# Graph attention on one core: the weights-row gathers moved behind the last residual of A on GpSimd's queue, and the B matmuls made to wait for them in four groups

## The chip, the cores and the metric

The kernel runs on one core of a Trainium2 chip. The metric is device time in microseconds (us) of the whole launch. Three runs of the kernel before took 432.70, 432.72 and 432.77 us, so the median is 432.72 us. Five compute engines work side by side, each with its own queue of instructions, and meet only at semaphores: TensorE (PE, with its weight loads shown apart as PEld), VectorE (DVE), ScalarE (ACT), GpSimd (POOL) and SyncE (SP), which here only starts DMAs. GpSimd starts DMAs too, the indirect ones, which gather rows by a table of indices.

## The reference

There are 2048 nodes with 128 features. `X` is 2048 x 128, `A` is 2048 x 2048.

```python
XW = X @ W
s_col = XW @ a[0, :f];  s_row = XW @ a[0, f:]
den = exp(leaky_relu(s_row[:, None] + s_col[None, :], 0.01))
num = A @ den
att = where(num != 0, den / num, 0)
H = A @ (att @ XW)
out = layernorm(x + H)
```

## The kernel before, in words

The kernel sorts the nodes by their row score and, apart from that, by their column score. `den` is then a staircase: for most pairs of a block of rows and a block of columns, leaky_relu is linear, and the product with `A` splits into sums that need only a few coefficients. Only the blocks on the staircase's edge are multiplied out in full.

**Stage A** brings in `A` transposed, in the sorted order of its rows, as 32 half blocks of 128 x 1024 values in 32 bits (the code calls their number `n`, block `b = n // 2`, half `h = n % 2`; the text here says "half 23" and so on). Each half goes through four steps:

- GpSimd issues an indirect DMA that gathers it into one of the 11 places of a ring (L233, `fetch`). Half `n + 11` is fetched only once half `n` has left its place.
- ScalarE casts it to 16 bits, into `Ahi` (L432, semaphore `hi_done`).
- The residual, the half minus `Ahi`, goes into `Alo`: for two halves of three on VectorE (L718, `lo_dve`), and for every third (`n % LOS == LOS - 1` with `LOS = 3`, so halves 2, 5, ..., 20, 23, 26, 29) on GpSimd (L244, `lo_pool`). This is what "a residual of A" is in the title.
- TensorE multiplies it by `E`, in six matmuls a half (L347), after `wait_lo(pe, n)`, which wants the residuals of all halves up to `n`. That sum is `ps`, later `sums`.

`Alo` and `Ahi` of blocks 12 to 15 (halves 24 to 31) lie where the ring's places were. So the cast and the residual of these halves also wait until the places are vacated (`wait_vacated`): the casts of halves 24 and 25 want all residuals up to 22, those of 26 and 27 want them up to 24, those of 28 and 29 up to 26, and those of 30 and 31 up to 28. The residuals of 24 and 25 want them up to 21, of 26 and 27 up to 23, of 28 and 29 up to 25, of 30 and 31 up to 27. "Up to" takes in those on GpSimd.

**Stage C** begins when TensorE is through with half 31. It has 64 steps `t = 4 * J + c`, of 16 blocks `J` and 4 column parts `c`. In a step TensorE forms `num` (L379, L384, L386: two matmuls with `sums` and, between them, usually six with `Ahi`, `Alo` and `D`), ScalarE takes square, logarithm and exponential (L484, L486, L477), VectorE forms the leaky_relu, subtracts the logarithm and multiplies to give `att` (L738, L755, L746). Three steps later TensorE adds `xws[J]` times `att` to `B` (L357, in `add_bt(t)`; a matmul in 32 bits, which the trace shows as two). `xws` holds the rows of `XW` in the order of the column scores, 128 of them for each `J`. They are gathered from the scratch tensor `d_xw` in HBM by 16 indirect DMAs on GpSimd (L260), one for each `J`.

After stage C the 16 blocks of `B` are scattered back to HBM in the order of the row scores (L268, GpSimd), read again, and multiplied by `A` (L407). Then come the layernorm and the store.

What sets the order: each engine runs its queue in the order in which the code writes it. GpSimd has one queue for the fetches, its residuals, the gathers of L260 and the scatters of L268. In the loop over `n` the gathers stand at `n = 21` to `28` (`XWG = 21`), two at each `n`.

Of the kernel before, what the change touches and what calls it, by code (L numbers as in the profile page):

```python
# [7 lines left out]
FEAT = 128  # L8
# [4 lines left out]
NB = NODES // P  # L13
# [1 line left out]
BATCH = tuple((s, min(s + NB // 2, NS)) for s in range(0, NS, NB // 2))  # L15
CROW = 4
STAIR = 8
XWG = 21
LOS = 3
LATE = 12  # L20
R = 96
# [15 lines left out]
def graph_attention_layernorm(nc, xT, x, adjT, w, wT, a2, cst, before, ids, out):  # L37
# [17 lines left out]
    NC = N // W  # L55
# [4 lines left out]
    with ctx:  # L60
        def sb(name, shape, dt=F32):
            return ctx.enter_context(nc.sbuf_tensor(name, shape, dt))

        def sem(name):
            return ctx.enter_context(nc.semaphore(name))

        def dram(name, shape, dt=F32):
            return nc.dram_tensor(name, shape, dt, kind="Internal").ap()
# [7 lines left out]
        xws = sb("xws", [P, N])  # L76
# [11 lines left out]
        perm = sb("perm", [P, 2, 3, NB], U32)  # L88
# [48 lines left out]
        RG = len(ring)  # L137
# [12 lines left out]
        d_xw = dram("d_xw", [N, FEAT])  # L150
# [6 lines left out]
        names = """in_w in_x in_c p_wa wa_sb p_row p_col r_even r_odd row_c rcol_sb ccol_sb p_xw xw_sb xw_out  # L157
            const ramp flags flags_used ranked_sb hots p_place perm_r perm_c thr hot p_pre cmax crow_t crow_sb
            slots_ready mask_ready hi_done lo_dve lo_pool e_zero e_ready p_sums sums_hi sums_sb
            m_ready e_exp v d_z d_lz d_exp d_lo w_exp w_m w_hi w_lo xws_in r01_sb shift_sb num_ready  # L160
            lz_ready sq_done ln_done sub_done exp_done att_ready bt_added bt_sb b_t b_sb b_out
            b_in0 b_in1 bhi_done blo_done ht ht_sb h_t x_in var std y_ready stored""".split()
        names += [f"g{i}" for i in range(RG)]
        S = {n: sem(n) for n in names}
        block = ctx.enter_context(nc.Block())

        def wait_lo(engine, n):

            engine.wait_ge(S["lo_dve"], n + 1 - (n + 1) // LOS)
            if n + 1 >= LOS:  # L170
                engine.wait_ge(S["lo_pool"], (n + 1) // LOS)

        def wait_vacated(engine, n, part):

            if n // 2 >= LATE:
                wait_lo(engine, n // 2 * 2 - (2 if part is Ahi else 3))
# [7 lines left out]
        @block.sync  # L184
        def _(sp):
            sp.dma_start(wTs[:, :], wT).then_inc(S["in_w"], 16)
            sp.dma_start(a2s[:, :], a2).then_inc(S["in_w"], 16)
            sp.dma_start(xTs[:, :], xT).then_inc(S["in_x"], 16)
            sp.dma_start(ws[:, :], w).then_inc(S["in_x"], 16)
            sp.dma_start(tri[:, :], before).then_inc(S["in_c"], 16)  # L190
            sp.dma_start(idt[:, :, :], ids).then_inc(S["in_c"], 16)
            sp.dma_start(cstt[:, :], cst).then_inc(S["in_c"], 16)
            sp.wait_ge(S["xw_sb"], 1)
            sp.dma_start(d_xw.rearrange("(b p) f -> p b f", p=P), stage[:, 0:N].rearrange("p (b f) -> p b f", b=NB)
                         ).then_inc(S["xw_out"], 16)

            sp.wait_ge(S["bt_added"], NB * NC)
            sp.dma_start(xs.rearrange("p (b f) -> p b f", b=NB), x.rearrange("(b p) f -> p b f", p=P)).then_inc(S["x_in"], 16)

            sp.wait_ge(S["b_out"], 16 * NB)  # L200
            for g in range(2):
                sp.dma_start(Bs[:, g * N // 2:(g + 1) * N // 2].rearrange("p (b f) -> p b f", b=NB // 2),
                             d_b.rearrange("(b p) f -> p b f", p=P)[:, g * NB // 2:(g + 1) * NB // 2, :]).then_inc(S[f"b_in{g}"], 16)
            for c in range(NC):
                sp.wait_ge(S["y_ready"], c + 1)
                sp.dma_start(out.rearrange("(b p) f -> p b f", p=P)[:, 4 * c:4 * c + 4, :],
                             y[:, 4 * c:4 * c + 4, :]).then_inc(S["stored"], 16)
            sp.wait_ge(S["stored"], 16 * NC)

        @block.gpsimd  # L210
        def _(pool):
            nc.gpsimd.memset(ident[:, :], 1.0).then_inc(S["const"], 1)
            nc.gpsimd.memset(epst[:, 0:1], EPS).then_inc(S["const"], 1)
            nc.gpsimd.memset(epst[:, 1:2], TINY).then_inc(S["const"], 1)
            nc.gpsimd.memset(E[:, :, :, :], 0.0).then_inc(S["e_zero"], 1)
            pool.wait_ge(S["const"], 3)
            nc.gpsimd.affine_select(out=ident[:, :], in_=ident[:, :], compare_op=ALU.is_equal, fill=0.0, base=0,
                                    pattern=[[-1, P]], channel_multiplier=1).then_inc(S["const"], 1)

            nc.gpsimd.iota(ramp16[:, :], pattern=[[1, N]], base=0, channel_multiplier=0,  # L220
                           allow_small_or_imprecise_dtypes=True).then_inc(S["ramp"], 1)
            nc.gpsimd.memset(onesb[:, :], 1.0).then_inc(S["const"], 1)
            pool.wait_ge(S["perm_r"], 1)

            rows = adjT.rearrange("k (h i) -> (k h) i", h=2)

            def fetch(n):
                b, h = divmod(n, 2)
                if n == RG - NG - 1:
                    pool.wait_ge(S["xw_out"], 16)  # L230
                if n >= RG:
                    wait_lo(pool, n - RG)
                nc.gpsimd.indirect_dma_start(  # L233
                    out=ring[n % RG], out_offset=None, in_=rows,
                    in_offset=bass.IndirectOffsetOnAxis(ap=perm[:, 0, h, b:b + 1], axis=0)).then_inc(S[f"g{n % RG}"], 16)

            for n in range(RG):
                fetch(n)
            for n in range(2 * NB):
                b, h = divmod(n, 2)  # L240
                if n % LOS == LOS - 1:
                    pool.wait_ge(S["hi_done"], n + 1)
                    wait_vacated(pool, n, Alo)
                    nc.gpsimd.tensor_tensor(Alo[:, b, h * H:(h + 1) * H], ring[n % RG], Ahi[:, b, h * H:(h + 1) * H],  # L244
                                            ALU.subtract).then_inc(S["lo_pool"], 1)
                if n + RG < 2 * NB:
                    fetch(n + RG)
                if n == STAIR + 1:

                    pool.wait_ge(S["mask_ready"], 1)  # L250
                    pool.wait_ge(S["w_exp"], 1)
                    w3 = tmp[0:R, :].rearrange("p (b j) -> p b j", b=NB)
                    nc.gpsimd.tensor_tensor(w3, w3, mask[0:R, :].unsqueeze(2).to_broadcast([R, NB, P]), ALU.mult
                                            ).then_inc(S["w_m"], 1)
                if n == XWG:
                    pool.wait_ge(S["perm_c"], 1)
                if XWG <= n < XWG + NB // 2:

                    for b in range(2 * (n - XWG), 2 * (n - XWG + 1)):
                        nc.gpsimd.indirect_dma_start(  # L260
                            out=xws[:, b * FEAT:(b + 1) * FEAT], out_offset=None, in_=d_xw,
                            in_offset=bass.IndirectOffsetOnAxis(ap=perm[:, 1, 2, b:b + 1], axis=0)).then_inc(S["xws_in"], 16)


            for b in range(NB):
                if b % 4 == 0:
                    pool.wait_ge(S["b_sb"], b // 4 + 1)
                nc.gpsimd.indirect_dma_start(  # L268
                    out=d_b, out_offset=bass.IndirectOffsetOnAxis(ap=ranku[:, b:b + 1], axis=0),
                    in_=Bn[:, b * FEAT:(b + 1) * FEAT], in_offset=None).then_inc(S["b_out"], 16)  # L270
# [8 lines left out]
        def _(pe):  # L279
# [5 lines left out]
            for i in (1, 0):  # L285
# [7 lines left out]
                for b in range(NB):  # L293
                    if i and b % 4 == 0:
                        h, c = divmod(b // 4, 2)
# [35 lines left out]
            for n in range(2 * NB):  # L331
# [11 lines left out]
                b, h = divmod(n, 2)  # L343
# [7 lines left out]

            def add_bt(t):
                J, c = divmod(t, NC)
                if c == 0:
                    pe.wait_ge(S["xws_in"], 16 * NB)
                pe.wait_ge(S["att_ready"], t + 1)
                nc.tensor.matmul(bt[c], xws[:, J * FEAT:(J + 1) * FEAT], att[c], start=(J == 0), stop=(J == NB - 1)  # L357
                                 ).then_inc(S["bt_added"], 1)
# [11 lines left out]
            for J in range(NB):  # L370
                lo, hi1 = ends_of(J)
                for c in range(NC):
                    t = J * NC + c
# [24 lines left out]
            for c in range(NC - LAG, NC):  # L398
                add_bt((NB - 1) * NC + c)
                transpose_b(c - 1)  # L400
# [113 lines left out]
        def _(dve):  # L514
# [170 lines left out]
            def leaky_relu(i):  # L685

                z, _, s1 = batch(i)
                dve.wait_ge(S["d_z"], s1)
                V.scalar_tensor_tensor(z, z, SLOPE, z, ALU.mult, ALU.max).then_inc(S["d_lz"], 1)
# [119 lines left out]
```

## Time and profile before

| | |
|---|---|
| median of three runs | 432.72 us |
| profiled execution, its own time | 432.18 us |
| its span, first to last instruction | 430.4 us |
| mean granted TensorE clock | 0.845 |
| TensorE matmuls busy | 296.5 us (69%) |
| VectorE busy | 251.3 us (58%) |
| ScalarE busy | 195.5 us (45%) |
| GpSimd busy | 103.1 us (24%) |
| indirect DMAs of L260: count, time from issue to landing | 16, 2.6 us |

The span is 430.4 us and the execution's own time 432.18 us, so 1.78 us lie around the span. The busy shares are averages over stages with different limits. GpSimd's 24% is nearly all in stage A and between C and the last product with `A`. The granted clock is that of TensorE as a share of 2.4 GHz: 1.00 is the upper of its two levels and 0.50 the lower, and a stretch with 0.7 has both in it.

### The profile page before, as it was taken

Reading aid. Unit: us, or ns where it says so; the run is one execution under the profiler, and the core shown is the slowest. Engines: PE = TensorE matmul, PEld = TensorE weight load, DVE = VectorE, ACT = ScalarE, POOL = GpSimd, SP = SyncE. Lnnn points to the kernel's source line nnn. Section 1 sums busy time; section 2 is a strip of 40 time slices with the busy share of each in tenths; the row PEclk is TensorE's granted clock in tenths of the full one; section 3 lists DMA queues with packets and bytes.
Section 4 is the critical chain, followed back from the end, with each engine's and each line's share of the span. In section 5 each row is a group of like instructions: output and inputs, shape, how many; then the busy total and the mean of one; then the engine's idle time right before and its main releaser. Section 6 shows DMA issues by size and latency. Waiting matters only on the chain.

```text
span 430.4 us, 5170 instructions
## 1 busy us (share of the span) xinstructions
PE 296.5 (69%) x1466; PEld 145.1 (34%) x1466; DVE 251.3 (58%) x468; ACT 195.5 (45%) x294; POOL 103.1 (24%) x86
## 2 busy tenths in 40 slices
PE   4863122863456555669999999999999700699950
PEld 2463111631122222324444444444444300244420
DVE  0759977477688413196888888876888500201036
ACT  1210013142697413187878787857878800100020
POOL 4000057563766788200000000000000174000000
PEclk9985555967588988689999999999999965699985
DMA  3030049732246511000000000000000052200002
GB/s 121 0 97 4 2 150 376 250 128 88 81 148 190 164 37 36 14 0 0 2 1 2 0 2 0 0 2 0 2 0 0 8 152 75 59 2 1 0 24 73
DMA packets 13445, 24.65 MB, mean 57 GB/s; under 512 B 1648, under 2 KB 8176, under 8 KB 13296
## 3 DMA queue, kind: packets, MB, share of 16 engines
q0 software_dynamic: 5632, 18.88, 13.5%
q1 hardware_dynamic: 7792, 5.50, 4.4%
q8 instruction: 12, 0.20, 0.2%
q14 instruction: 9, 0.07, 0.1%
HBM read 21.23 MB, written 3.15 MB: 57 GB/s over the span
## 4 chain that ended last, share of the span: by engine, by line
PE 51%; DVE 19%; POOL 12%; ACT 7%; issue 5%; DMA 4%; POOLq 0%; SPq 0%; ACTq 0%; DVEq 0%
PE ps L384 18%; PE ps L357 11%; PE ps L407 10%; POOL xws L260 4%; POOL d_b L268 3%; PE ps L347 3%; DVE Alo L718 2%; DVE D L547 2%; PE ps L290 2%; POOL Alo L244 2%; DVE D L549 2%; PE ps L379 2%; PE ps L386 2%; DMA Ahi<-adjT,perm 2%; ACT tmp L458 1%
## 5 line engine op out<-in xcount | busy, mean ns | idle before, releaser
L347 PE MATMUL ps<-Ahi,E 128*96 128x512 f16 x128 | 54.9, 490 | 53.9 <-POOL Alo L244 30.5
L384 PE MATMUL ps<-Ahi,D 128*128 x248 | 85.3, 383 | 0.7 <-issue 0.4
L357 PE MATMUL ps<-stage,xws 128*128 128x512 f32 x128 | 65.8, 595 | 3.7 <-DVE stage L746 3.7
L755 DVE TENSOR_TENSOR tmp<-crow,tmp 128x512 f32<-128x512 f32 x64 | 44.2, 691 | 30.4 <-ACT tmp L486 30.4
L407 PE MATMUL ps<-Ahi,D 128*128 128x512 f16 x128 | 39.7, 389 | 25.0 <-DVE D L763 25.0
L268 POOL DMA_INDIRECT d_b<-crow,ranku x16 | 15.4, 961 | 170.8 <-ACT crow L493 166.2
L484 ACT ACTIVATE tmp<-ps 128x512 f32<-128x512 f32 x64 | 38.0, 594 | 29.0 <-PE ps L386 29.0
L384 PE MATMUL ps<-Alo,D 128*128 x124 | 47.4, 382 | 0.0
L347 PEld LDWEIGHTS ps<-Ahi,E 128*96 128x96 f16 x128 | 19.9, 156 | 81.1 <-issue 57.0
L486 ACT ACTIVATE tmp<-tmp,epst 128x512 f32<-128x512 f32 x64 | 46.2, 722 | 2.1
L477 ACT ACTIVATE tmp<-tmp,ebias 128x512 f32<-128x512 f32 x64 | 45.3, 708 | 0.2 <-DVE tmp L755 0.2
L746 DVE SCALAR_TENSOR_TENSOR stage<-ps,tmp 128x512 f32<-128x512 f32 x64 | 43.7, 683 | 0.2 <-ACT tmp L477 0.2
L384 PEld LDWEIGHTS ps<-Ahi,D 128*128 x248 | 24.1, 97 | 44.0 <-issue 23.2
L347 PE MATMUL ps<-Alo,E 128*96 128x512 f16 x64 | 31.3, 489 | 0.0
L233 POOL DMA_INDIRECT Ahi<-adjT,perm x12 | 15.2, 1270 | 58.5 <-DVE rs L576 51.4
L407 PEld LDWEIGHTS ps<-Ahi,D 128*128 128x128 f16 x128 | 12.8, 100 | 40.8 <-DVE D L763 25.3
L407 PE MATMUL ps<-Alo,D 128*128 128x512 f16 x64 | 24.8, 388 | 0.0
L738 DVE SCALAR_TENSOR_TENSOR crow<-crow,shift,rrow 128x512 f32<-128x512 f32 x32 | 23.8, 742 | 0.1
L357 PEld LDWEIGHTS ps<-stage,xws 128*128 128x128 f32 x128 | 19.6, 193 | 12.1 <-issue 3.7
L738 DVE SCALAR_TENSOR_TENSOR crow<-stage,shift,rrow 128x512 f32<-128x512 f32 x32 | 23.7, 742 | 0.0
L432 ACT CAST Ahi<-Ahi 128x1024 f16<-128x1024 f32 x12 | 12.5, 1040 | 21.7 <-POOL Alo L244 17.8
L718 DVE TENSOR_TENSOR Alo<-Ahi 128x1024 f16<-128x1024 f32 x8 | 10.9, 1357 | 19.0 <-ACT Ahi L432 18.9
(166 smaller groups left out, 407.2 us busy)
## 6 DMA issues: line engine op xcount, KB each, us to landing
tmp<-xT SPq DMA_DIRECT2D x1, 1024.0 KB, 4.9
d_xw<-stage SPq DMA_DIRECT2D x1, 1024.0 KB, 5.1
xws<-d_b SPq DMA_DIRECT2D x2, 512.0 KB, 4.6
out<-crow SPq DMA_DIRECT2D x4, 256.0 KB, 2.3
xws<-d_xw,perm POOLq DMA_INDIRECT x16, 2.6
d_b<-crow,ranku POOLq DMA_INDIRECT x16, 2.2
Ahi<-adjT,perm POOLq DMA_INDIRECT x12, 5.4
Alo<-adjT,perm POOLq DMA_INDIRECT x11, 5.6
```

The costliest lines, as they stand in the source:

```text
L268: nc.gpsimd.indirect_dma_start(out=d_b, out_offset=bass.IndirectOffsetOnAxis(ap=ranku[:, b:b + 1], axis=0), in_=Bn[:, b * FEAT:(b + 1) * F ...
L347: mm = nc.tensor.matmul(ps[0:R, c, :], E[:, e, b, :], a[:, b, c * W:(c + 1) * W], start=(b == 0 and i == 0), stop=(b == NB - 1 and i == 2))
L357: nc.tensor.matmul(bt[c], xws[:, J * FEAT:(J + 1) * FEAT], att[c], start=(J == 0), stop=(J == NB - 1)).then_inc(S["bt_added"], 1)
L384: nc.tensor.matmul(num[c], D[:, d, bass.ds(slot, 1), :], a[:, bass.ds(k, 1), o:o + W], start=False, stop=False, skip_group_check=True)
L407: mm = nc.tensor.matmul(bt[c], B16[:, d, k, :], a[:, k, c * W:(c + 1) * W], start=(k == 0 and i == 0), stop=(k == NB - 1 and i == 2))
L477: nc.scalar.activation(L_t[c], L_t[c], ACT.Exp, bias=ebias[:, J:J + 1]).then_inc(S["exp_done"], 1)
L484: nc.scalar.activation(L_t[c], num[c], ACT.Square, scale=1.0 / 256).then_inc(S["sq_done"], 1)
L486: nc.scalar.activation(L_t[c], L_t[c], ACT.Ln, bias=epst[:, 1:2]).then_inc(S["ln_done"], 1)
L718: V.tensor_tensor(Alo[:, b, h * H:(h + 1) * H], ring[n % RG], Ahi[:, b, h * H:(h + 1) * H], ALU.subtract).then_inc(S["lo_dve"], 1)
L738: V.scalar_tensor_tensor(lz_t[t % 2], r01[c // 2][:, c % 2 * W:(c % 2 + 1) * W], shift[:, J:J + 1], rrow[:, c * W:(c + 1) * W], ALU.add, A ...
L746: V.scalar_tensor_tensor(att[c], num[c], 1.0 / 256, L_t[c], ALU.mult, ALU.mult).then_inc(S["att_ready"], 1)
L755: V.tensor_tensor(L_t[c], lz_t[t % 2], L_t[c], ALU.subtract).then_inc(S["sub_done"], 1)
```

## The change

The 16 gathers leave the loop over the halves and stand behind it, so that GpSimd issues them one after another when it is through with its last residual (half 29) and the loop. The semaphore `xws_in`, which counted all 16, becomes four, one for every four gathers (`XG = 4`). TensorE, which waited for all 16 at the first column part of every `J`, now waits at `J = 0, 4, 8, 12` for the group of that `J` alone.

```diff
-XWG = 21
+XG = 4
...
-        ... w_hi w_lo xws_in r01_sb ...
+        ... w_hi w_lo r01_sb ...
-        names += [f"g{i}" for i in range(RG)]
+        names += [f"g{i}" for i in range(RG)] + [f"xws_in{i}" for i in range(NB // XG)]
...
-                if n == XWG:
-                    pool.wait_ge(S["perm_c"], 1)
-                if XWG <= n < XWG + NB // 2:
-
-                    for b in range(2 * (n - XWG), 2 * (n - XWG + 1)):
-                        nc.gpsimd.indirect_dma_start(
-                            out=xws[:, b * FEAT:(b + 1) * FEAT], out_offset=None, in_=d_xw,
-                            in_offset=bass.IndirectOffsetOnAxis(ap=perm[:, 1, 2, b:b + 1], axis=0)).then_inc(S["xws_in"], 16)
-
+            pool.wait_ge(S["perm_c"], 1)
+            for b in range(NB):
+                nc.gpsimd.indirect_dma_start(
+                    out=xws[:, b * FEAT:(b + 1) * FEAT], out_offset=None, in_=d_xw,
+                    in_offset=bass.IndirectOffsetOnAxis(ap=perm[:, 1, 2, b:b + 1], axis=0)).then_inc(S[f"xws_in{b // XG}"], 16)
...
-                if c == 0:
-                    pe.wait_ge(S["xws_in"], 16 * NB)
+                if t % (NC * XG) == 0:
+                    pe.wait_ge(S[f"xws_in{J // XG}"], 16 * XG)
```

GpSimd's queue at the end of stage A, before. `L244` are its residuals (of halves 20, 23, 26 and 29 in this order), `L233` the fetches of halves of A, `L260` the gathers:

```order
L244 TENSOR_TENSOR Alo<-stage,Ahi 128x1024 [waits hi_done]
L233 DMA stage<-adjT,perm 128x1024 [waits lo_pool,lo_dve]
L260 DMA xws<-d_xw,perm 128x128 [waits perm_c]
L260 DMA xws<-d_xw,perm 128x128 x3
L244 TENSOR_TENSOR Alo<-Alo,Ahi 128x1024 [waits hi_done]
L260 DMA xws<-d_xw,perm 128x128 x6
L244 TENSOR_TENSOR Alo<-Ahi 128x1024 [waits lo_pool,lo_dve,hi_done]
L260 DMA xws<-d_xw,perm 128x128 x6
L244 TENSOR_TENSOR Alo<-stage,Ahi 128x1024 [waits lo_pool,lo_dve,hi_done]
```

The same place now, where the gathers are `L257` and the scatters of `B` that follow are `L264`:

```order
L244 TENSOR_TENSOR Alo<-stage,Ahi 128x1024 [waits hi_done]
L233 DMA stage<-adjT,perm 128x1024 [waits lo_pool,lo_dve]
L244 TENSOR_TENSOR Alo<-Alo,Ahi 128x1024 [waits hi_done]
L244 TENSOR_TENSOR Alo<-Ahi 128x1024 [waits lo_pool,lo_dve,hi_done]
L244 TENSOR_TENSOR Alo<-stage,Ahi 128x1024 [waits lo_pool,lo_dve,hi_done]
L257 DMA xws<-d_xw,perm 128x128 [waits perm_c]
L257 DMA xws<-d_xw,perm 128x128 x15
L264 DMA d_b<-crow,ranku 2048x128 [waits b_sb]
```

Between residuals 20 and 29 stood 4, 6 and 6 gathers; now the residuals follow one another, and all 16 gathers stand behind the last one. The fetch in front (of half 31, the last) did not move.

TensorE's queue where it adds `B` for the first column part of `J = 2`, before:

```order
L386 MATMUL ps<-sums,wgt 128x256
L357 MATMUL ps<-stage,xws 128x512 [waits att_ready,xws_in]
L367 TENSOR_LOAD lohi
L367 ISA x2
L368 TENSOR_LOAD lohi
L368 ISA x2
L379 MATMUL ps<-sums,wgt 128x256 [waits att_ready]
```

The same rows now (`L353` is the matmul into `B`):

```order
L382 MATMUL ps<-sums,wgt 128x256
L353 MATMUL ps<-stage,xws 128x512 [waits att_ready]
L363 TENSOR_LOAD lohi
L363 ISA x2
L364 TENSOR_LOAD lohi
L364 ISA x2
L375 MATMUL ps<-sums,wgt 128x256 [waits att_ready]
```

No matmul moved. The wait for the gathers is gone here, and at 12 of its 16 places; at the other four it names a group of four gathers.

## Rows read from the trace of the kernel before

**Rows 1.** The page, the chain that ended last, shares of the span by line:

```profile
PE ps L384 18%; PE ps L357 11%; PE ps L407 10%; POOL xws L260 4%; POOL d_b L268 3%; PE ps L347 3%; DVE Alo L718 2%; DVE D L547 2%; PE ps L290 2%; POOL Alo L244 2%; DVE D L549 2%; PE ps L379 2%; PE ps L386 2%; DMA Ahi<-adjT,perm 2%; ACT tmp L458 1%
```

**Rows 2.** Waits, 140 to 200 us (waiting line, awaited: us in total, times, longest):

```profile
PE ps L347 <- POOL Alo L244: 18.1, 4, 5.7
ACT Ahi L432 <- POOL Alo L244: 17.8, 3, 8.1
```

**Rows 3.** Timeline, GpSimd (start us, us, engine, line, instruction [idle before <-releaser]):

```profile
142.60 2.28 POOL L244 TENSOR_TENSOR Alo<-stage,Ahi 128x1024 f16<-128x1024 f32 x1
145.65 0.96 POOL L233 DMA_INDIRECT stage<-adjT,perm  x1 [0.77 <-POOL Alo L244]
...
151.88 2.14 POOL L244 TENSOR_TENSOR Alo<-Alo,Ahi 128x1024 f16<-128x1024 f32 x1
...
161.94 2.14 POOL L244 TENSOR_TENSOR Alo<-Ahi 128x1024 f16<-128x1024 f32 x1
164.24 0.96 POOL L260 DMA_INDIRECT xws<-d_xw,perm  x1 [0.16 <-issue]
...
168.86 1.96 POOL L260 DMA_INDIRECT xws<-d_xw,perm  x1 [0.30 <-issue]
...
173.32 2.14 POOL L244 TENSOR_TENSOR Alo<-stage,Ahi 128x1024 f16<-128x1024 f32 x1
```

**Rows 4.** Timeline, ScalarE and VectorE at the end of stage A:

```profile
147.21 1.22 DVE L718 TENSOR_TENSOR Alo<-Alo,Ahi 128x1024 f16<-128x1024 f32 x1
...
154.12 1.04 ACT L432 CAST Ahi<-Ahi 128x1024 f16<-128x1024 f32 x1 [7.14 <-POOL Alo L244]
...
156.15 1.23 DVE L718 TENSOR_TENSOR Alo<-Alo,Ahi 128x1024 f16<-128x1024 f32 x1 [7.72 <-ACT Ahi L432]
...
166.57 1.99 ACT L432 CAST Ahi<-stage 128x1024 f16<-128x1024 f32 x2 [0.39 <-issue]
...
167.64 2.36 DVE L718 TENSOR_TENSOR Alo<-stage,Ahi 128x1024 f16<-128x1024 f32 x2 [1.16 <-ACT Ahi L432]
```

**Rows 5.** Timeline, TensorE: matmuls after a short idle time, and where stage C starts:

```profile
122.08 0.42 PE L347 MATMUL ps<-Ahi,E 128*96 128x512 f16 x1 [1.28 <-DVE Alo L718]
...
145.03 0.39 PE L347 MATMUL ps<-Ahi,E 128*96 128x512 f16 x1 [2.87 <-POOL Alo L244]
...
148.70 0.38 PE L347 MATMUL ps<-Ahi,E 128*96 128x512 f16 x1
...
182.04 0.38 PE L347 MATMUL ps<-Ahi,E 128*96 128x512 f16 x1
...
189.78 1.10 PE L357 MATMUL ps<-stage,xws 128*128 128x512 f32 x2 [3.10 <-DVE stage L746]
```

**Rows 6.** Windows (stretch, its us, busy us and instructions of each engine, granted clock, DMA):

```profile
154.10:159.80 5.70, 5.61 (x18) 2.77 (x18) 1.23 (x1) 1.99 (x2) 4.41 (x5) 0.72 0.14 35
175.60:182.40 6.80, 6.80 (x19) 3.26 (x19) 0.82 (x2) 1.07 (x2) 0.00 (x0) 0.59 0.01 2
189.70:195.00 5.30, 4.78 (x11) 1.85 (x12) 4.32 (x7) 2.89 (x6) 0.00 (x0) 0.68 0.00 0
200.00:240.00 40.00, 40.00 (x170) 18.23 (x169) 32.73 (x51) 32.40 (x51) 0.00 (x0) 1.00 0.01 1
```

**Rows 7.** Timeline, 106 to 119 us: GpSimd and VectorE at the same time:

```profile
106.04 3.62 POOL L253 TENSOR_TENSOR tmp<-tmp,mask 96x2048 f32<-96x2048 f32 x1
107.41 3.33 DVE L718 TENSOR_TENSOR Alo<-Alo,Ahi 128x1024 f16<-128x1024 f32 x1 [2.60 <-ACT Ahi L432]
111.62 2.28 DVE L708 TENSOR_TENSOR wgt<-tmp,wgt 32x2048 f16<-32x2048 f32 x1 [0.87 <-ACT wgt L447]
112.61 3.27 POOL L244 TENSOR_TENSOR Alo<-Ahi 128x1024 f16<-128x1024 f32 x1 [0.61 <-ACT Ahi L432]
116.50 1.23 DVE L689 SCALAR_TENSOR_TENSOR tmp<-tmp 128x1024 f32<-128x1024 f32 x1 [2.60 <-ACT tmp L458]
116.66 1.90 POOL L233 DMA_INDIRECT Ahi<-adjT,perm  x1 [0.77 <-POOL Alo L244]
117.64 1.22 DVE L718 TENSOR_TENSOR Alo<-Alo,Ahi 128x1024 f16<-128x1024 f32 x1
```

**Rows 8.** The instructions of line L260, their transfers:

```profile
DMA to landing us min/median/max: 2.4/2.6/3.7
```

More of the change, by code:

```diff
@@ L159, in graph_attention_layernorm @@
             slots_ready mask_ready hi_done lo_dve lo_pool e_zero e_ready p_sums sums_hi sums_sb
-            m_ready e_exp v d_z d_lz d_exp d_lo w_exp w_m w_hi w_lo xws_in r01_sb shift_sb num_ready
+            m_ready e_exp v d_z d_lz d_exp d_lo w_exp w_m w_hi w_lo r01_sb shift_sb num_ready
             lz_ready sq_done ln_done sub_done exp_done att_ready bt_added bt_sb b_t b_sb b_out
             b_in0 b_in1 bhi_done blo_done ht ht_sb h_t x_in var std y_ready stored""".split()
-        names += [f"g{i}" for i in range(RG)]
+        names += [f"g{i}" for i in range(RG)] + [f"xws_in{i}" for i in range(NB // XG)]
         S = {n: sem(n) for n in names}
```

## The prediction

> **What bounds the kernel now.** I read the chain that ended last first. TensorE's lines of stage C and of the last product lead it, but one entry does not fit: the gathers of L260 hold 4% of the span, and GpSimd's residuals L244 another 2% [rows 1]. The gathers' data is first used in stage C, at 189.78 us, so their issue should be on no path. The waits from 140 to 200 us say how they come onto it: TensorE waits 18.1 us for residuals on GpSimd, and ScalarE's casts 17.8 us for the same [rows 2]. GpSimd's timeline closes the argument. After the fetch at 145.65 it has nothing before it but gathers, and the residuals of halves 23, 26 and 29 begin at 151.88, 161.94 and 173.32 only because they stand behind 4, 6 and 6 gathers [rows 3]. The next cast starts 0.10 us after the residual of half 23 is done (154.02), VectorE's next residual after the cast [rows 4]. So from 146.6 to 175.5 us GpSimd's queue bounds the kernel. From 182.42 us (the end of 182.04 + 0.38 [rows 5]) stage C follows, in which TensorE is busy 40.00 of 40.00 us [rows 6].
>
> **The change, part by part.**
>
> *Gathers out of the way.* The stretches that hold gathers are 146.61 to 151.88 (5.27 us), 154.02 to 161.94 (7.92) and 164.08 to 173.32 (9.24), 22.4 us together [rows 3]. They do not come back in full, since the casts and VectorE's residuals, which now run in their shadow, are late next. I follow them.
>
> Residual 23 is ready when the fetch ends, at 146.61; its cast is long done. Before, VectorE had the residuals of halves 24 and 25 until 148.43 [rows 4]. They now meet GpSimd's. The rows on such meetings: GpSimd's residual at 112.61 took 3.27 us instead of 2.14 and ended 1.98 us after VectorE's subtraction did (113.90); VectorE's residual at 107.41 took 3.33 instead of 1.22 and ended 1.08 after GpSimd's multiplication (109.66) [rows 7]. One waits for the other. Residual 24 on VectorE ends near 147.30 (25 begins 147.21), so residual 23 ends at 147.30 + 1.98 = 149.3 if it gets in between the two, and at 148.43 + 1.98 = 150.4 if it does not. With no such cost it would end at 146.61 + 2.14 = 148.75.
>
> The Trainium skill has this as a rule (SBUF — State Buffer, "Who interferes with whom"): VectorE's second read port is GpSimd's only one, and a VectorE instruction with two SBUF inputs and a GpSimd instruction that reads SBUF exclude each other for the whole instruction. The trace agrees, with the 3.27 and 3.33 us above. By the rule residual 23 ends at 149.3 or 150.4, and the case without a cost falls away.
>
> From there, in the later of the two cases: casts 26 and 27 from 150.5, 1.99 us for two [rows 4], so 151.5 and 152.5. Residual 26 on GpSimd from 151.6 to 153.7. VectorE's 27 waits for it and ends near 154.8. Casts 28 and 29 from 153.8 to 155.8. VectorE's 28 to 156.0. Residual 29 starts then on GpSimd and ends at 158.0. Casts 30 and 31 end at 157.2 and 158.1. VectorE's 30 waits for GpSimd and ends at 159.1, 31 at 160.3. All arrivals of halves are old: half 31 was issued at 145.65.
>
> TensorE needs (148.70 - 145.03)/17 = 0.216 us a matmul at the upper clock [rows 5], 1.30 for a half. It was done with half 22 at 149.08. From the end of residual 23 nine halves are left, 54 x 0.216 + 0.17 = 11.8 us. It would start half 26 at 154.3 (ready 153.7), 27 at 155.6 (154.8), 28 at 156.9 (156.0), 29 at 158.2 (158.0), 30 at 159.5 (159.1), 31 at 160.8 (160.3). Each is ready by 0.2 to 0.9 us, so TensorE itself is late next. It ends between 149.3 + 11.8 = 161.1 and 150.4 + 11.8 = 162.2. I take 161.8, nearer the later end, as the margins are thin. Against 182.42 that saves 20.6 us.
>
> *The clock.* The saving assumes 1.00 from 149 us on. Before, the clock stood at 0.72 for the halves after the first stall and 0.59 after the third [rows 6], each after 5 us or more without work. After 1.28 us (at 122.08), and even after 2.87 (at 145.03), TensorE went on with matmuls of 0.4 us, the upper level [rows 5]. Only one gap of 0.2 to 1.3 us is left here (149.08 to the end of residual 23). So I count the clock at nothing. If it falls all the same, the price is between 0 and 54 x 0.216 = 11.7 us; one stretch like that of 154.10 to 159.80, whose 18 matmuls took 5.70 us instead of 18 x 0.216 + 0.17 = 4.06, costs 1.6 us.
>
> *Gathers in their new place.* POOL is free of residual 29 at 157.0 to 158.0. A gather costs 0.96 us and 0.30 between two, so 1.26, but one that started under VectorE's residuals took 1.96 [rows 3]. Taking 2.26 for each, the fourth starts at 158.2 + 3 x 2.26 = 165.0 and lands after 2.6 to 3.7 us [rows 8], at 167.6 to 168.7. `add_bt(0)` came 189.78 - 182.42 = 7.36 us after the end of stage A [rows 5], which is now 169.2. The first group is in time by 0.5 to 1.6 us; at 1.26 a gather by over 4. VectorE's 51 instructions in 40 us, three a step, make 17 steps, 2.35 us each [rows 6]. So the second group is needed 16 steps later, near 207, and the sixteenth gather starts by 158.2 + 15 x 2.26 = 192.1. Cost 0. Above it: if gathers cost VectorE their own time at the start of C, where there is no slack, it is four times 0.96, 3.8 us. Nothing in the rows says so: residuals 30 and 31 took 2.36 for two with gathers under them [rows 4]. After that VectorE is busy 32.73 of 40 [rows 6] and can give 7 us in 40.
>
> *Fewer waits on TensorE.* Twelve waits go that were long fulfilled; the engine was busy 40.00 of 40.00 with them there [rows 6]. An engine without idle time has none to give back, and nothing is added that could cost. So 0.
>
> *The rest.* Stage C and what follows keep their lengths and move forward as a block. Its own half-clock stretch (0.68 from 189.70 to 195.00 [rows 6]) comes after the 3.10 us wait for the first `att`, which stays; it could change by 1.6 us either way.
>
> **Sum.** 432.18 - 20.6 = 411.6 for the profiled execution. The median of the runs is 0.54 higher, so 412.1.
>
> **Rivals.**
>
> *The clock falls in the closed-up end of stage A.* For it: at 0.2 us of margin a small delay makes gaps, and the clock was at 0.72 and 0.59 in these very halves. Against: the gaps of 1.3 us that did not lower it. One stretch gives 413.7, two 415.3, all nine halves at the lower level 412.1 + 11.7 = 423.8.
>
> *The first group is late or disturbs VectorE.* Four gathers of 2.26 and a late landing leave only 0.5 us. Another 1 to 4 us here gives 413 to 416.
>
> *Something else holds the casts.* If the casts of 26 to 31 need more than the residuals (an arrival, a place), half of the 20.6 would go: 422. The casts' only wait in the rows is GpSimd (17.8 us in 3).
>
> *Starved gathers, slower than before.* Gathers wait for VectorE (1.96 and 1.90 us). VectorE is busy 82% of stage C. If a gather only goes ahead when VectorE stands still for a while, none is issued until TensorE stops at the group's wait and VectorE runs dry. Then four go, 3 x 1.26 + 2.6 = 6.4 us, and four groups cost 25.6, against 20.6 saved: 437, and the clock's falls (1.6 us or more each) would bring it to 444. It decides from 5.15 us a group. Against it: at 116.66 an indirect DMA under two VectorE instructions back to back ended at 118.56, 0.83 after the first of them (117.73) and before the second (118.86) [rows 7]. It needs only the seam.
>
> The Trainium skill warns of this (SBUF — State Buffer, the "DVE blocks DMA" trap): GpSimd cannot write descriptors while VectorE is in a two-port performance mode. It excepts subtractions of two tensors. The trace differs in part, since the subtractions of L718 did delay a gather to 1.96 us. By the trap taken at its worst the time is that of the starved gathers; by the row it is the forecast.
>
> **How the numbers follow.** Forecast 0.74, with its own range of 410.3 to 414. Falling clock 0.13. First group 0.06. Something else 0.04. Starved gathers 0.03. The range 409.5 to 417 takes in the forecast, up to three lower-clock stretches and the late group, and on its lower side a stage C that starts without its half-clock stretch; it leaves out some 0.1. What a measurement of this kernel can tell from no change is about 0.2%, 0.9 us. Faster 0.96, the same 0.01, slower 0.03.
>
> **What would show it.** On GpSimd's timeline residuals 23, 26 and 29 end near 150, 154 and 158, with no gather between. The waits of TensorE for L244 after 145 us fall from 15 us to about 1. Stage C's first matmul stands near 161.8, the first matmul into `B` near 169 with its wait put down to VectorE and not to a DMA. The steps keep their 2.35 us. I am wrong if the clock is well below 1.00 between 150 and 162, if TensorE waits for VectorE's residuals there, or if a wait ends with a gather's landing.

## The result, and the profile after

The changed kernel takes 419.65 us (median of four runs, 419.47 to 420.14), the kernel before 432.71 us in the same session. The ratio is 0.9708, 95% interval 0.9686 to 0.9729. The gain is 13.1 us where 20.6 were forecast, and the time lies above the range given. The profiled execution took 419.58 us, with a span of 417.8.

GpSimd's timeline at the end of stage A, where lines carry new numbers (L257 is the gather, L264 the scatter, L343 TensorE's matmul of stage A, L353 the one into `B`, L375, L380 and L382 those of `num`, L480 ScalarE's square, L714 VectorE's residual). It answers to [rows 3]:

```profile
146.51 0.96 POOL L233 DMA_INDIRECT stage<-adjT,perm  x1 [0.77 <-POOL Alo L244]
147.49 2.13 POOL L244 TENSOR_TENSOR Alo<-Alo,Ahi 128x1024 f16<-128x1024 f32 x1
151.91 2.13 POOL L244 TENSOR_TENSOR Alo<-Ahi 128x1024 f16<-128x1024 f32 x1 [2.29 <-DVE Alo L714]
156.22 2.22 POOL L244 TENSOR_TENSOR Alo<-stage,Ahi 128x1024 f16<-128x1024 f32 x1 [2.18 <-ACT Ahi L428]
158.59 1.78 POOL L257 DMA_INDIRECT xws<-d_xw,perm  x1
...
178.83 0.94 POOL L257 DMA_INDIRECT xws<-d_xw,perm  x1 [0.30 <-issue]
```

The residuals follow one another within 11 us instead of 24, and the 16 gathers run behind them, from 158.6 to 179.8 us, one in 1.25 us. TensorE's waits from 140 to 163 us, which answer to [rows 2]:

```profile
PE ps L343 <- POOL Alo L244: 2.9, 1, 2.9
PE ps L343 <- DVE Alo L714: 1.4, 1, 1.4
```

The 18.1 us for GpSimd have become 2.9, and those lie ahead of half 20. Stage A's last matmul ends at 162.97 us (162.59 + 0.38). The first fetch of this execution began 0.89 us later than before (58.17 against 57.28). Counted from it, stage A ends after 104.8 us instead of 125.1, so 20.3 us are saved there.

Then stage C. The windows (stretch, its us, then busy us of TensorE, its weight loads, VectorE, ScalarE and GpSimd, granted clock, DMA) answer to [rows 6]:

```profile
163.00:170.30 7.30, 4.20 (x20) 1.91 (x20) 6.60 (x13) 7.20 (x12) 5.59 (x6) 1.00 0.18 47
170.30:182.50 12.20, 8.75 (x21) 2.43 (x22) 4.27 (x7) 3.72 (x7) 7.34 (x8) 0.72 0.19 48
190.00:230.00 40.00, 40.00 (x170) 18.14 (x168) 32.72 (x52) 32.47 (x51) 0.00 (x0) 1.00 0.00 1
```

In 12.2 us TensorE ran 21 matmuls, where some 50 are usual, and VectorE and ScalarE were busy for a third of it. What happened is in the timeline of TensorE and ScalarE:

```profile
172.05 0.71 ACT L473 ACTIVATE tmp<-tmp,ebias 128x512 f32<-128x512 f32 x1
...
173.79 0.63 PE L380 MATMUL ps<-Alo,D 128*128 x1
174.84 0.59 PE L380 MATMUL ps<-Ahi,D 128*128 x1 [0.41 <-issue]
175.57 0.37 PE L382 MATMUL ps<-sums,wgt 96*128 96x256 f16 x1 [0.15 <-issue]
...
178.81 0.63 PE L380 MATMUL ps<-Ahi,D 128*128 x1
181.17 0.60 ACT L480 ACTIVATE tmp<-ps 128x512 f32<-128x512 f32 x1 [8.41 <-remote]
181.26 0.38 PE L380 MATMUL ps<-Ahi,D 128*128 x1 [1.82 <-issue]
```

ScalarE's L480 of step 4 waits for the matmul L382 of that step. It ended at 175.94, and L480 began at 181.17, 5.2 us later; further on the same pair is 0.05 us apart (L382 ends at 186.70, L480 begins at 186.75). The ends of matmuls are modelled, but TensorE started several more behind this one, the last of them at 178.81, so it had long been done. "remote" is how the profile names a wait for which it finds no engine whose end released it. TensorE itself stutters: "issue" is idle time in which it waited for nothing shown. Both recover at 181.2, about when the last gather, issued at 178.83, should have landed by the 2.6 us of [rows 8] (an estimate, as this trace gives no landing for it). From stage C's first matmul to the first scatter of `B` it took 165.39 us (163.06 to 328.45) instead of 159.33 (182.32 to 341.65), so 6.1 us more. After that the steps are the old ones, 40.00 us busy of 40.00.

### The profile page after: what moved, and what is told of

It is laid out like the page before. It is cut to its first block, busy times and chain, and to the rows that moved or that the text cites. A ratio compares the mean times of both kernels' runs of the same rounds, so it can differ in the third digit from the quotient of the medians.

```text
span 417.8 us, 5158 instructions
## 1 busy us (share of the span) xinstructions
PE 295.9 (71%) x1466; PEld 143.9 (34%) x1466; DVE 255.3 (61%) x468; ACT 195.5 (47%) x294; POOL 102.1 (24%) x86
## 4 chain that ended last, share of the span: by engine, by line
PE 57%; DVE 22%; ACT 7%; POOL 5%; issue 5%; DMA 3%; POOLq 0%; SPq 0%; ACTq 0%; DVEq 0%
PE ps L380 20%; PE ps L353 12%; PE ps L403 10%; PE ps L343 5%; POOL d_b L264 3%; DVE Alo L714 3%; DVE D L543 2%; PE ps L286 2%; PE ps L375 2%; PE ps L382 2%; DVE D L545 2%; ACT tmp L454 1%; DVE tmp L685 1%; PE ps L297 1%; DVE D L559 1%
## 5 line engine op out<-in xcount | busy, mean ns | idle before, releaser
L380 PE MATMUL ps<-Ahi,D 128*128 x248 | 86.5, 386 | 2.9 <-issue 2.6
L343 PE MATMUL ps<-Ahi,E 128*96 128x512 f16 x128 | 50.6, 458 | 39.1 <-DVE Alo L714 25.4
L353 PE MATMUL ps<-stage,xws 128*128 128x512 f32 x128 | 67.0, 605 | 3.6 <-issue 2.9
L480 ACT ACTIVATE tmp<-ps 128x512 f32<-128x512 f32 x64 | 38.1, 595 | 35.2 <-PE ps L382 26.8
L264 POOL DMA_INDIRECT d_b<-crow,ranku x16 | 15.5, 970 | 153.3 <-ACT crow L489 148.7
L380 PE MATMUL ps<-Alo,D 128*128 x124 | 47.9, 386 | 0.4 <-issue 0.3
L380 PEld LDWEIGHTS ps<-Ahi,D 128*128 x248 | 24.2, 98 | 48.7 <-issue 28.1
L343 PEld LDWEIGHTS ps<-Ahi,E 128*96 128x96 f16 x128 | 18.5, 144 | 63.0 <-issue 35.3
L233 POOL DMA_INDIRECT Ahi<-adjT,perm x12 | 15.2, 1270 | 59.4 <-DVE rs L572 52.3
L343 PE MATMUL ps<-Alo,E 128*96 128x512 f16 x64 | 29.1, 455 | 0.0
L353 PEld LDWEIGHTS ps<-stage,xws 128*128 128x128 f32 x128 | 19.6, 193 | 11.5 <-issue 3.3
L503 ACT COPY rrow<-ps 128x512 f32<-128x512 f32 x4 | 2.3, 586 | 42.4 <-PE ps L403 42.4
L714 DVE TENSOR_TENSOR Alo<-Ahi 128x1024 f16<-128x1024 f32 x8 | 13.4, 1677 | 11.2 <-ACT Ahi L428 11.0
```

The source lines that it names most:

```text
L264: nc.gpsimd.indirect_dma_start(out=d_b, out_offset=bass.IndirectOffsetOnAxis(ap=ranku[:, b:b + 1], axis=0), in_=Bn[:, b * FEAT:(b + 1) * F ...
L343: mm = nc.tensor.matmul(ps[0:R, c, :], E[:, e, b, :], a[:, b, c * W:(c + 1) * W], start=(b == 0 and i == 0), stop=(b == NB - 1 and i == 2))
L380: nc.tensor.matmul(num[c], D[:, d, bass.ds(slot, 1), :], a[:, bass.ds(k, 1), o:o + W], start=False, stop=False, skip_group_check=True)
L480: nc.scalar.activation(L_t[c], num[c], ACT.Square, scale=1.0 / 256).then_inc(S["sq_done"], 1)
L714: V.tensor_tensor(Alo[:, b, h * H:(h + 1) * H], ring[n % RG], Ahi[:, b, h * H:(h + 1) * H], ALU.subtract).then_inc(S["lo_dve"], 1)
```

## The experiments

Two theories stood at the start. Theory 1: the gathers in flight hold up stage C. Theory 2: the place in the program does. The second run below paces the gathers; it is called the paced kernel, and most later runs build on it. The runs come from several sessions; the kernel before took 432.46 to 432.79 us in each, so their times are compared as they are.

**Plain load.** No gather on GpSimd.

```diff
+            sp.wait_ge(S["perm_c"], 1)
+            sp.dma_start(xws ..., d_xw ...).then_inc(S["xws_in0"], 16)
...
-            for b in range(NB):
-                nc.gpsimd.indirect_dma_start(out=xws..., in_=d_xw, ...)
```

> The changed kernel without any gather on GpSimd: xws is filled by one plain DMA on SyncE as soon as its place is free (it leaves out the sorting of the rows of XW). In the changed kernel ScalarE stands still from 172.8 to 181.2 us, TensorE's steps 4 and 5 are ragged, and both recover when the last gather must have landed (issued at 178.8). Theory 1, gathers in flight hold up the engines of stage C: the standstill is gone and the time is 419.65 - 6.5, so about 413, within 1 us of the 412.1 forecast. Theory 2, the standstill belongs to the place in the program (start of the second block J, where TensorE loads the loop bounds into registers and jumps): it stays, and the time is about 419.5.

412.44 us (411.03 to 413.13), ratio 0.9538 [0.9519, 0.9557]. No wait in stage C is "remote". This run leaves out the sorting of the rows. The standstill went with the gathers, and the forecast for the rest of the change holds.

**Paced groups.**

```diff
             for b in range(NB):
+                if b and b % XG == 0:
+                    pool.wait_ge(S["bt_added"], NC * b - 8)
```

> The changed kernel, with groups 1, 2 and 3 of the gathers held back on GpSimd until eight steps before TensorE needs them, so that only four gathers, over by about 166 us, run at the start of stage C and the others run in three bursts of 5 us later. Theory 1 in its simple form (any gather beside stage C costs): each burst shows its own standstill of some us, so about the 419.6 of the changed kernel, or more. Theory 1 with a threshold (only a long train of gathers builds something up, since the first ten ran beside stage C at no cost): no standstill, about 413. Theory 2 (place in the program): the standstill at step 4 stays, about 419.5.

411.40 us (410.66 to 411.88), ratio 0.9513 [0.9496, 0.9529]. This version does the whole work and is faster than both kernels, than the changed one by 8.2 us. Its windows of stage C, the second with the usual fall of the clock after the wait for the first `att`, the third with group 1 of the gathers in it:

```profile
161.50:169.00 7.50, 4.39 (x21) 2.15 (x22) 6.67 (x12) 7.40 (x12) 1.03 (x2) 1.00 0.07 20
169.00:182.00 13.00, 12.70 (x46) 5.16 (x45) 9.80 (x16) 9.26 (x16) 0.00 (x0) 0.87 0.00 0
182.00:200.00 18.00, 18.00 (x77) 8.24 (x76) 14.94 (x24) 14.46 (x23) 3.78 (x4) 1.00 0.05 15
```

TensorE is busy 18.00 of 18.00 us with four gathers beside it. So neither the place nor gathers as such cost anything; theory 2 falls, and theory 1 needs its threshold. Stage A ends 104.6 us after the first fetch (161.35 against 56.80), 20.6 us less than before.

**One wait for all 16**, the second part of the change undone:

```diff
-                if t % (NC * XG) == 0:
-                    pe.wait_ge(S[f"xws_in{J // XG}"], 16 * XG)
+                if c == 0:
+                    for g in range(NB // XG):
+                        pe.wait_ge(S[f"xws_in{g}"], 16 * XG)
```

> The changed kernel with the second part of the change undone: TensorE waits for all 16 gathers before the first matmul into B and at every block J, as before. The last gather lands at about 181.3, the first matmul into B stands at 170.3 now. If the wait alone counts, the time is 419.65 + 11 less the standstill of 6.5 that would lie inside this wait: about 424. If the standstill comes in addition, about 430. Under theory 2 the standstill comes after the wait, so 430.

424.63 us (two runs), ratio 0.9815 [0.9782, 0.9847]. The first matmul into `B`:

```profile
180.71 2.05 PE L354 MATMUL ps<-stage,xws 128*128 128x512 f32 x2 [14.67 <-DMA xws<-d_xw,perm]
```

It waits for the last gather and the standstill lies inside that wait, as the lower figure assumed. The groups are worth 5.0 us beside the new place of the gathers; against the 412.4 us of the plain load, where nothing stands still, they would be worth 12.2.

**Twelve gathers more**, into a place that nobody reads, behind the 16:

```diff
+            pool.wait_ge(S["p_sums"], 2)
+            for b in range(12):
+                nc.gpsimd.indirect_dma_start(out=spare[...], in_=d_xw, ...).then_inc(S["spare_in"], 16)
```

> The changed kernel with 12 more gathers of the same rows into a place that nobody reads, right behind the 16. GpSimd's train then ends at about 195 instead of 179.8. Theory 1: the standstill of ScalarE ends with the last landing, near 196.5, and the time grows by about 15, to 434. Theory 1 weaker (gathers slow the engines for a bounded time): 420 to 430. Theory 2: no change, 419.6.

435.92 us (434.16 to 438.42), 16.3 over the changed kernel, for a train 15 us longer. ScalarE's waits (us in total, times, longest):

```profile
ACT tmp L487 <- remote: 24.2, 3, 15.6
```

In the next runs the paced kernel carries something extra behind group 0, from about 163 us on.

**24 plain DMAs by SyncE** of as many bytes:

```diff
+            for k in range(24):
+                sp.dma_start(spare[...], d_xw[k % 12 * P:(k % 12 + 1) * P, :]).then_inc(S[f"sp_in{k % 12}"], 16)
```

> The paced kernel (411.4 us) and, from the start of stage C on, 24 plain DMAs of 64 KB each from the same scratch tensor, issued back to back by SyncE into a place that nobody reads. They bring as many bytes and as many completions as 24 gathers, with no work on GpSimd. Theory A (the traffic of the transfers and their completions on the semaphores hold up TensorE and ScalarE): a standstill as with a train of gathers, 425 us or more. Theory B (it needs GpSimd issuing the DMAs): no standstill, 411 to 413.

412.20 us. Theory A falls: neither the bytes nor the completions do it. (They were issued in 12.4 us, about twice as fast as the gathers.)

**24 gathers on GpSimd**, the control, and **24 gathers of 32 rows**:

```diff
+                if b == XG:
+                    pool.wait_ge(S["p_sums"], 2)
+                    for k in range(24):
+                        extra(pool, k)    # an indirect gather of 128 (then 32) rows into spare
```

> The paced kernel with a train of 24 gathers of 128 rows behind group 0 on GpSimd, from 163 to 193 us, into a place that nobody reads. This is the control. The train of 28 gathers in the earlier run cost 24.5 us over the paced kernel. Both theories: a standstill that ends near 194, and about 434 us. If it stays near 411, the groups' own place (first matmul into B, waits on four semaphores) has a part in it.

> The same train of 24 gathers, but each of 32 rows instead of 128: the same number of instructions on GpSimd, a quarter of the rows, descriptors and bytes. Theory B1 (what holds up the others grows with the descriptors that GpSimd writes): the standstill is gone or a quarter, 411 to 417. Theory B2 (it goes by the number of DMAs and their completions): as with 128 rows, near 434 less what the shorter train saves.

436.13 us and 435.68 us. A quarter of the rows changes nothing, so it goes by the number of gathers. ScalarE in the run with 32 rows, and between its two rows the matmul L399 of TensorE that the second of them waits for:

```profile
172.89 0.60 ACT L497 ACTIVATE tmp<-ps 128x512 f32<-128x512 f32 x1 [2.92 <-remote]
184.84 0.37 PE L399 MATMUL ps<-sums,wgt 96*128 96x256 f16 x1 [2.21 <-issue]
197.41 0.60 ACT L497 ACTIVATE tmp<-ps 128x512 f32<-128x512 f32 x1 [22.56 <-remote]
```

Of the 22.56 us TensorE's own ragged issue took the first part, up to 185.21; the signal was late by the other 12.2.

**24 gathers, one a step.** The same, each behind `pool.wait_ge(S["bt_added"], k + 1)`.

> The paced kernel with the same 24 extra gathers of 128 rows, but only one in each step of stage C (one in 2.4 us instead of one in 1.25 us). If the rate decides (something fills up when gathers come faster than it drains): no standstill, 411 to 413. If each gather beside stage C costs a fixed time that the first ten only hid: as the control, near 434.

417.24 us, between the two figures: 5.8 us over the paced kernel. The one standstill stands where group 1 met the spaced gathers and made them a train again. GpSimd and ScalarE there (gathers of the group are L274, the extra ones L217):

```profile
187.37 0.95 POOL L217 DMA_INDIRECT E<-d_xw,perm  x1 [1.43 <-PE ps L370]
189.75 0.95 POOL L217 DMA_INDIRECT E<-d_xw,perm  x1 [1.43 <-PE ps L370]
191.00 0.94 POOL L274 DMA_INDIRECT xws<-d_xw,perm  x1 [0.30 <-issue]
...
197.26 0.94 POOL L217 DMA_INDIRECT E<-d_xw,perm  x1 [0.30 <-issue]
199.82 0.60 ACT L497 ACTIVATE tmp<-ps 128x512 f32<-128x512 f32 x1 [4.44 <-remote]
200.10 0.95 POOL L217 DMA_INDIRECT E<-d_xw,perm  x1 [1.90 <-remote]
```

GpSimd's own wait for a matmul of TensorE was late as well, so it is TensorE's signals that come late, whoever waits for them. Here seven in a row were enough (from 189.75 to 197.26), behind seven that came one in 2.4 us or slower. At the next group, five in a row behind eleven spaced ones cost nothing that shows.

**24 memsets, and 24 direct DMAs, on GpSimd** in the train's place:

```diff
-            nc.gpsimd.indirect_dma_start(...)
+            nc.gpsimd.memset(spare[:, 0:1024], 0.0)...
+            # or: nc.gpsimd.dma_start(spare[...], d_xw[k % 12 * P:(k % 12 + 1) * P, :])...
```

> The paced kernel with 24 memsets on GpSimd (128 x 1024 values of 32 bits, some 1 us each) in the place of the train of 24 gathers. Theory C1 (any busy GpSimd queue beside stage C holds up TensorE): near 434. Theory C2 (it is the issue of a DMA by GpSimd): no standstill, 411 to 413.

> The same train of 24 DMAs on GpSimd's queue, but direct ones of 128 rows that lie together, with no table of indices. If every DMA that GpSimd issues does it: near 434, as with gathers. If the reading of the index table or the indirect form is what counts: 411 to 413.

412.61 us and 412.60 us. Neither costs more than 1.2 us over the paced kernel. The two rows from GpSimd's timeline:

```profile
162.87 24.20 POOL L217 MEMSET E<- 128x1024 f32 x24
```

```profile
163.70 12.85 POOL L217 DMA_DIRECT2D E<-d_xw  x24
```

The direct ones came even faster, one in 0.54 us. Their train was over at 176.6, while the control's runs to 193.4; but in the control ScalarE's first "remote" wait ended at 171.08 already, so a standstill would have shown. So it takes the indirect form on GpSimd. What a direct train of 30 us would do was not run.

**The train beside the last product.**

```diff
+            pool.wait_ge(S["blo_done"], 2)
+            for k in range(24):
+                extra(pool, k)
```

> The paced kernel with the train of 24 gathers not in stage C but beside the last product with A, where TensorE runs 192 matmuls of fixed operands and few semaphores pass. Theory D1 (any TensorE work suffers under the train): the product grows by 10 to 20 us, the time is 420 to 432. Theory D2 (only stage C's steps suffer, whose matmuls take their addresses from registers in a loop): the product keeps its 45 us and the time stays at 411 to 413.

427.60 us (two runs), 16.2 over the paced kernel: D1 holds, D2 falls. TensorE's L419 is the last product, and ScalarE's L519 waits for a quarter of it; the train runs from 350.50 to 380.3 us:

```profile
361.07 0.59 PE L419 MATMUL ps<-Ahi,D 128*128 128x512 f16 x2
364.65 0.59 ACT L519 COPY rrow<-ps 128x512 f32<-128x512 f32 x1 [15.68 <-remote]
...
369.27 0.38 PE L419 MATMUL ps<-Alo,D 128*128 128x512 f16 x1
370.28 0.60 PE L419 MATMUL ps<-Ahi,D 128*128 128x512 f16 x2 [0.63 <-issue]
372.41 0.38 PE L419 MATMUL ps<-Alo,D 128*128 128x512 f16 x1 [1.52 <-issue]
...
376.63 0.58 PE L419 MATMUL ps<-Alo,D 128*128 128x512 f16 x1 [2.22 <-issue]
```

TensorE starts at the lower clock, as in the paced kernel, and from 353.7 us on keeps its pitch of 0.216 us a matmul beside the gathers up to the fifteenth, until 369 us; then it issues a matmul or two in 2 us until the train is over. It has no semaphore to wait for there. Its signal is late earlier than its issue is ragged: the quarter's last matmul is the first of the pair at 361.07 (counted at that pitch) and ends near 361.45, beside the ninth gather, and ScalarE starts 3.2 us later; in the paced kernel the same pair is 0.04 us apart.

**Two fixed blocks a step in place of the register loop, with the train and without it.**

```diff
-                    with pe.Fori(lo, hi1) as k:
+                    for k in range(min(NB - 1 - J, NB - 2), min(NB - 1 - J, NB - 2) + 2):
```

> The kernel with the paced groups and the train of 24 gathers in stage C, where TensorE's loop with bounds from registers is replaced by two fixed blocks a step (it leaves out the staircase: the blocks multiplied are not the ones that the data ask for, and four of the steps have six matmuls instead of nine). With no train I expect 409 from it, 2.4 us less than the paced kernel for the four longer steps. Theory D2: the standstill goes with the loop, 408 to 412. Theory D3 (what suffers is the semaphore traffic of TensorE in general, fixed or not): 425 to 434, with ScalarE waiting for TensorE's increments as before.

> The control of the run with two fixed blocks a step and a train (432.0 us): the same fixed blocks, the paced groups, no train (it leaves out the staircase in the same way). 409 us, 2.4 under the paced kernel for its four longer steps. Then the train costs 23 us with fixed blocks as with the register loop (24.7), and the loop has no part in it. If the control itself is slow, 420 or more, that conclusion falls.

432.04 us with it (427.34 to 433.15) and 408.65 us without. The train costs 23.4 us, about the 24.7 that it costs the register loop. The loop has no part in it.

**Two trains of eight, and filler work between the gathers.**

```diff
-                if b and b % XG == 0:
+                if b == 2 * XG:
                     pool.wait_ge(S["bt_added"], NC * b - 8)
```

> The paced kernel with two trains of eight gathers instead of four of four: groups 0 and 1 back to back from 157 us, groups 2 and 3 eight steps before TensorE needs group 2. The changed kernel issued ten gathers beside a smooth stage C before the first step went wrong. If a train has to be longer than about ten: no standstill, 411 to 412. If eight are enough beside full-speed TensorE work (the second train): one standstill of some us, 414 to 418.

```diff
+                if b >= XG:
+                    if b > XG:
+                        pool.wait_ge(S["filled"], b - XG)
+                    nc.gpsimd.memset(spare[:, 0:1152], 0.0).then_inc(S["filled"], 1)
```

> The changed kernel with a memset of 1.1 us on GpSimd ahead of each of the gathers 4 to 15, so that they come one in about 2.5 us, and no wait on TensorE's semaphores between them. If the rate of the gathers decides: no standstill, 411 to 413. If the paced kernel owes its gain to something else (the wait itself, or that no more than four come in a row): a standstill as in the changed kernel, 416 to 420.

412.35 us (412.29 to 412.61), ratio 0.9540 [0.9517, 0.9562], and 412.41 us (411.40 to 413.21), ratio 0.9531 [0.9506, 0.9557]. Neither has a "remote" wait. Eight in a row cost nothing that shows, and the filler alone, with no wait on TensorE, gives the gain: the rate and the length of the train decide. The length that is free is no fixed number, though, as the seven in a row behind spaced gathers show.

## Why the prediction was wrong

- *What bounds stage A* was right. With the gathers gone from between the residuals stage A became 20.3 us shorter in the changed kernel and 20.6 in the paced one; 20.6 were forecast.
- *Who is late next* was right: from half 20 on TensorE ran without a gap to 162.97 us, from 149 us on at a clock of 1.00. The way there was not the predicted one. Residual 23 did not wait for VectorE. It ran from 147.49 to 149.62, and VectorE's residual 24, though it began first, took 3.79 us, to 150.72. TensorE did not notice, as halves 20 to 22 had run in part at the lower clock and it was behind by then. The Trainium skill (SBUF — State Buffer, "Who interferes with whom") lets issue order decide which of the two is blocked. By the recorded starts of these two it was the later one that went ahead, and the measurement decides; but GpSimd's fetch of 146.51 was still running when VectorE's residual began, so whether VectorE ever had the ports is open.
- *The clock*, counted at nothing, fell ahead of the stretch that was looked at. Behind the 2.88 us wait ahead of half 20 it was 0.50 from 145.80 to 148.60, and seven matmuls took 2.89 us instead of 1.51; behind a wait of 2.87 us at the same place it stayed at the upper level before, and in the paced kernel. It cost little: at the upper level TensorE met the other engines' limits instead (the paced kernel waits 0.37 and 0.34 us for GpSimd's residuals 26 and 29), and stage A of the paced kernel is only 0.2 us shorter. That 20.3 came so near 20.6 is in part luck. TensorE began half 23 near 151.2, which is 150.3 if counted from the first fetch as before, so where the forecast had it (149.3 to 150.4), but because of the lower clock and not for a wait for residual 23.
- *The first group in time* was right: the first matmul into `B` came 7.37 us after the end of stage A (170.34 - 162.97), against 7.36 before, and it is no gather that it waits for: the fourth was issued at 163.18, and VectorE's first `att` was done at 170.19.
- *"Gathers in their new place. Cost 0"* was the step that failed. I asked only whether the gathers arrive in time and whether they disturb VectorE, and took it that they cost TensorE nothing while they are in time. The trace of before could not show the price: beside a TensorE at work it had no more than six indirect DMAs in a row. It had eleven in a row (the fetches from 57.28 us) and sixteen (the scatters from 341.65), but TensorE was busy for 0.95 of 14.30 and 2.29 of 20.00 us there. Measured, the step costs 6.1 us in stage C, in which the train made TensorE's signals late and its issue ragged; with no gather on GpSimd, or with the gathers paced, the time is 412.4 and 411.4 us, and 412.1 was forecast. My bound above zero, 3.8 us, was put on the wrong engine.
- *The starved gathers* were the wrong way round. But for the first, under residual 31, the gathers ran at 0.94 to 1.29 us beside VectorE, hardly held up, and TensorE was held up. The Trainium skill (SBUF — State Buffer, "Who interferes with whom") says that TensorE never waits on anyone. That is said of the ports of SBUF, and no run here tells whether it fails for them, but it is no ground for calling GpSimd's DMA issue free for TensorE, as the 6.1 us show.
- *The sum.* Against the profiled execution that was forecast, 411.6, the measured one has 8.0 us more: 6.1 in stage C, 0.9 from a later first fetch, 0.6 behind the first scatter (89.35 against 88.75), 0.3 in stage A and 0.2 between the stages. The later fetch is no part of the change: the paced kernel began 0.5 us earlier than before.

Shown by the runs: a train of indirect gathers on GpSimd's queue makes TensorE's signals late and TensorE's issue ragged, the price grows with the number of gathers in the train and not with their rows, and spacing them removes it (twelve at one in 2.3 us cost nothing that shows). Not shown: what GpSimd and TensorE share there. The pattern, smooth for some nine to fifteen gathers and then signals late by up to 12.2 us until about the end of the train, looks like something that fills faster than it drains; that is argued only. Nor do these runs tell whether the recording of the profile takes part in it.

## What to carry to other kernels

When a block of DMA issues is moved, ask not only when its data is needed and whose buffers it frees, but which engines run at full speed beside it in the new place, and whether the trace has ever shown such a train beside them; if not, put a price on it or pace it. Gathers that are needed one after another can be issued that way, a few at a time behind the consumer's own progress: here one wait on `bt_added` ahead of each group of four gave back 8.2 us. In the profile, look for waits named "remote", and for idle time named "issue" on an engine that has nothing to wait for.

## What the runs showed of the hardware

- A train of 24 indirect DMAs on GpSimd's queue, one in 1.25 us (1.17 with 32 rows each), cost 24.7 us beside stage C with 128 rows each and 24.3 with 32 rows, and 16.2 beside the last product. 24 direct DMAs on the same queue, one in 0.54 us, 24 plain ones by SyncE and 24 memsets of 1.0 us cost 0.8 to 1.2 us over the paced kernel, which is about the spread of the runs (410.66 to 411.88 for the paced kernel alone).
- Eight indirect DMAs in a row, or four in a row and then twelve at one in 2.3 us, cost no more than that. Seven in a row behind seven that came one in 2.4 us or slower did: ScalarE waited 4.4 us once, and that run is 5.8 us over the paced kernel.
- Where a residual of GpSimd and one of VectorE met, VectorE's was held up (3.79 us) although it had begun 0.56 us earlier (146.93 and 147.49), the other way round than at 112.61 us before [rows 7]; a fetch of GpSimd's was running from 146.51 to 147.47.
- After a wait of TensorE of 2.87 or 2.88 us at the same place, its clock stayed at 1.00 in the kernel before and in the paced one and was 0.50 for 2.8 us in the changed one.
